# Retention block and expert layer on one core: group norm and residual of the last two items on another engine, one item stored in two parts, filler products and a new order at the end

## The chip, the core and the metric

The kernel runs on one NeuronCore of a Trainium2 chip. Five engines work side by side and meet only at semaphores: TensorE (PE) multiplies, VectorE (DVE) and ScalarE (ACT) do elementwise work and may read PSUM, GpSimd (POOL) does elementwise work in SBUF and issues the adding DMAs, SyncE (SP) issues the plain DMAs. The metric is the time of one launch in microseconds, the median of several runs.

## What is computed

The reference, cut to what matters. An item is one of the 8 batch entries of 512 tokens with 128 features. Four layers of the block run over 8 items, so the kernel counts 32 items, n = 0 to 31, with n = 8·layer + batch entry. The last three are 29, 30 and 31.

```python
xn = layernorm(x)                                   # (8, 512, 128)
def block(h, p):                                    # 4 layers
    r = retention(h, wk)                            # scores, row norm, times v
    a, gate = split(r @ w1 + b1)
    m = (a * silu(gate)) @ w2 + b2
    m = (m - mean(m over the item)) / sqrt(var + eps) * gg + gb    # group norm
    y = m + h                                       # residual
    f = gelu(y @ wf1 + bf1) @ wf2 + bf2
    return layernorm(f + y) * lg + lb
s = block x 4 (xn)
g = silu(moe(xn))                                   # 8 experts, one chosen per token
out = x + s * g
```

## The kernel before

The program is a software pipeline of steps. Step s handles the retention of item s, the gated product and group norm of item s-1, and the GELU product of item s-2; the layer norm of item s-3 follows. Tiles of the expert layer are woven between. Steps 0 to 29 are regular. After them each engine runs a hand-written list, its function `ending`, and since every engine runs its list strictly in that order, the lists fix which wait stands in front of which work. All that the change touches lies in these five lists and in the functions they call, from about 441 us of the profiled span on.

For an item n of the ending the chain is this. TensorE: `query`, `states`, `scores`, `outputs` (retention), `u_by_feature` (transposes), `late_value` and `late_gate` (first weight), `second_weight` (into bank 6; for item 31 `last_second_weight` in two halves into `pair`). Then the statistics of the group norm: sums over the free axis (ACT `group_sums` for items 29 and 30, DVE `last_sum_stats` and `last_group_sums` for 31), the sum over partitions by a product with a constant matrix (`late_means`), mean and variance on DVE (`late_gn_moments`), the power -1/2 on POOL (`gn_pow`), scale and shift per feature on DVE (`gn_shift`, three instructions of one column: gn_sc, gn_d, gn_bi). ACT's `residual` or `last_residual` writes scale·m + shift into y_sb, DVE's `y_residual` or `last_y` adds the input h (hT). TensorE's `gelu_first` reads y_sb, ACT's `gelu` reads its result, TensorE's `gelu_second` adds y and the second product (the tiles bank <- ident,y_sb and bank <- all_f,G_sb), and DVE takes the layer norm's statistics (`z_stats`, `z_moments`). POOL's `ln_pow` makes the factor.

For batch entries 0 to 4 the layer norm's result goes through `z_hat` (DVE, half of the rows), `layernorm` (ACT, the other half), POOL's `rows_scale` and `rows_shift` (times lg, plus lb), POOL's `scale` (times the SiLU of the expert layer, which lies in y_tok) and POOL's `store`, a DMA that adds to `out`, which was filled with x beforehand. For 5, 6 and 7, DVE prepares with `weigh("scale"|"bias"|"x", b)` the tensors g·lg, g·lb and x + g·lb, and after the statistics finishes with `centre` and `finish`, four passes of 128 columns each. Entry 5 is stored by an adding DMA of POOL, 6 and 7 by plain DMAs of SP, the last of which starts after `finish(31, 4, (2, 3))`.

The means of an item over all of its elements come, for the last items, as three columns from four products (mean, mean of squares, eps, minus the mean), so that DVE needs two instructions to the variance:

```python
mm(means_bank(n)[:, 0:1], mean[:, :], gs[:, 0:1], start=True, stop=True)        # L1619
mm(means_bank(n)[:, 1:2], mean[:, :], gs[:, 1:2], start=True, stop=False)       # L1620
mm(means_bank(n)[:, 1:2], mean_of[:, :], eps_sb[:, :], start=False, stop=True)  # L1621
mm(means_bank(n)[:, 2:3], less[:, :], gs[:, 0:1], start=True, stop=True)        # L1622
```

## Time and profile before

| | |
|---|---|
| median of 3 runs | 499.3 us (499.13 to 499.41) |
| the profiled execution | 499.69 us, of which the profile's span is 497.9 us |
| PE busy | 471.7 us (95%) |
| DVE busy | 369.5 us (74%) |
| ACT busy | 262.9 us (53%) |
| POOL busy | 258.5 us (52%) |

The profile gives for every instruction its start and duration, for idle time what ended it, and for any stretch the busy time of each engine with the clock that was granted to TensorE (PEclk; 1.00 is 2.4 GHz, 0.50 is 1.2 GHz). Times in the rows count from the span's start. A matmul of float32 stands as two instructions, so x4 are two products. A product's listed duration includes the time that it needs to drain; the distance of two starts is what it costs TensorE.

### The profile page before, as it was taken

Reading aid. Unit: us, or ns where it says so; the run is one execution under the profiler, and the core shown is the slowest. Engines: PE = TensorE matmul, PEld = TensorE weight load, DVE = VectorE, ACT = ScalarE, POOL = GpSimd, SP = SyncE. Lnnn points to the kernel's source line nnn. Section 1 sums busy time; section 2 is a strip of 40 time slices with the busy share of each in tenths; the row PEclk is TensorE's granted clock in tenths of the full one; section 3 lists DMA queues with packets and bytes.
Section 4 is the critical chain, followed back from the end, with each engine's and each line's share of the span. In section 5 each row is a group of like instructions: output and inputs, shape, how many; then the busy total and the mean of one; then the engine's idle time right before and its main releaser. Section 6 shows DMA issues by size and latency. Waiting matters only on the chain.

```text
span 497.9 us, 9900 instructions
## 1 busy us (share of the span) xinstructions
PE 471.7 (95%) x3167; PEld 395.3 (79%) x3167; DVE 369.5 (74%) x1326; ACT 262.9 (53%) x551; POOL 258.5 (52%) x289
## 2 busy tenths in 40 slices
PE   7999889998999999999999999999999999999964
PEld 5787566676898898898889889888988988876643
DVE  4758878887777676777767777867777786776866
ACT  3823344444564546665454666454466654488623
POOL 4520188888544555444455554454555455664551
PEclk9999999999999999999999999999999999999967
DMA  9999911111611111111111111110111100066034
GB/s 265 234 136 114 397 33 39 38 40 36 129 65 59 38 65 60 60 44 36 55 40 65 60 60 44 60 38 32 66 60 59 40 11 12 13 169 65 0 28 79
DMA packets 47393, 36.62 MB, mean 74 GB/s; under 512 B 13336, under 2 KB 38752, under 8 KB 47312
## 3 DMA queue, kind: packets, MB, share of 16 engines
q1 hardware_dynamic: 41376, 28.93, 22.9%
q0 software_dynamic: 5440, 6.28, 5.7%
q10 hardware_dynamic: 528, 0.79, 0.5%
q8 instruction: 27, 0.44, 0.4%
q14 instruction: 22, 0.18, 0.1%
HBM read 16.27 MB, written 10.99 MB: 55 GB/s over the span
## 4 chain that ended last, share of the span: by engine, by line
PE 71%; POOL 11%; DVE 8%; issue 6%; DMA 2%; ACT 1%; SPq 0%; DVEq 0%; POOLq 0%
PE bank L1595 9%; PE bank L1494 7%; PE bank L1478 7%; POOL x_slots L512 6%; PE pair L1687 4%; PE pair L1678 4%; PE pair L1644 4%; PE bank L1698 4%; PE bank L1505 4%; PE bank L1506 4%; PE bank L1507 4%; PE pair L1689 3%; PE pair L1639 3%; PE bank L1593 2%; PE bank L1533 2%
## 5 line engine op out<-in xcount | busy, mean ns | idle before, releaser
L546 POOL TENSOR_TENSOR zhat<-zhat,all_lg 128x512 f32<-128x512 f32 x29 | 38.6, 1332 | 80.3 <-PE bank L1551 73.9
L1595 PE MATMUL bank<-all_f,G_sb 128*128 128x128 f32 x512 | 74.5, 279 | 0.0
L1595 PEld LDWEIGHTS bank<-all_f,G_sb 128*128 128x128 f32 x512 | 68.9, 196 | 1.8 <-issue 1.7
L772 ACT ACTIVATE y_sb<-bank,gn_bi,gn_sc 128x512 f32<-128x512 f32 x31 | 24.1, 779 | 87.0 <-DVE gn_bi L1344 87.0
L745 ACT ACTIVATE uT_h<-bank 128x512 fp32r<-128x512 f32 x30 | 17.9, 598 | 92.8 <-PE bank L1561 92.8
L467 POOL TENSOR_TENSOR ln_rs<-ln_ve,half_neg 128x4 f32<-128x4 f32 x31 | 32.7, 1055 | 35.3 <-DVE ln_ve L871 35.1
L1478 PEld LDWEIGHTS bank<-moe_w,h_T 128*128 128x128 f32 x312 | 39.5, 191 | 14.0 <-issue 14.0
L659 ACT ACTIVATE h_T<-bank,w_t 128x128 f32<-128x128 f32 x156 | 44.6, 373 | 4.9 <-PE bank L1494 4.9
L593 POOL DMA_INDIRECT y_rows<-yt,slot_info x39 | 40.9, 1050 | 11.1 <-POOL yt L590 11.1
L716 ACT ACTIVATE G_sb<-bank,all_par 128x512 f32<-128x512 f32 x62 | 41.7, 694 | 9.3 <-PE bank L1533 7.0
L537 POOL TENSOR_TENSOR gn_rs<-gn_ve,half_neg 128x1 f32<-128x1 f32 x32 | 19.4, 607 | 49.5 <-DVE gn_ve L1210 40.3
L1494 PE MATMUL bank<-xtT,w_t 128*128 128x128 f32 x312 | 43.2, 281 | 0.0
L1478 PE MATMUL bank<-moe_w,h_T 128*128 x312 | 42.0, 278 | 0.0
L1133 DVE TENSOR_TENSOR rs<-pair,floor_sb 128x4 f32<-128x4 f32 x32 | 5.2, 162 | 47.3 <-PE pair L1689 46.3
L590 POOL TENSOR_SCALAR yt<-yt,slot_info 128x128 f32<-128x128 f32 x39 | 23.7, 608 | 30.3 <-DVE yt L1375 30.3
L554 POOL TENSOR_TENSOR htok<-zhat,all_lb 128x512 f32<-128x512 f32 x29 | 37.9, 1309 | 2.3
L1494 PEld LDWEIGHTS bank<-xtT,w_t 128*128 128x128 f32 x312 | 37.9, 192 | 0.0
L1689 PE MATMUL pair<-S_sb,q_sb 128*128 128x129 f32 x192 | 37.1, 275 | 0.0
L512 POOL DMA_INDIRECT x_slots<-xn,pos x32 | 32.6, 1019 | 8.1 <-issue 8.1
L1593 PE MATMUL bank<-ident,y_sb 128*128 128x128 f32 x128 | 35.6, 278 | 0.9 <-ACT G_sb L716 0.9
L1505 PE MATMUL bank<-uT_h,all_w 128*128 128x512 f32 x60 | 33.4, 557 | 1.7 <-DVE uT_l L1198 1.1
L1678 PE MATMUL pair<-q_sb,hT 128*128 128x128 f32 x256 | 34.0, 276 | 0.2 <-ACT q_sb L756 0.2
(227 smaller groups left out, 1249.2 us busy)
## 6 DMA issues: line engine op xcount, KB each, us to landing
w_t<-moe_w SPq DMA_DIRECT2D x39, 258.0 KB
x_slots<-moe_w SPq DMA_DIRECT2D x1, 2515.5 KB, 22.9
xt<-x_slots SPq DMA_DIRECT2D x39, 64.0 KB, 1.8
x_sb<-in_L_attn_x SPq DMA_DIRECT2D x8, 256.0 KB, 5.7
moe_w<-in_L_ffn_w SPq DMA_DIRECT2D x1, 2048.0 KB, 21.1
moe_w<-y_rows SPq DMA_DIRECT2D x8, 256.0 KB, 4.7
out<-in_L_attn_x SPq DMA_DIRECT2D x1, 1536.0 KB, 15.9
out<-moe_w POOLq DMA_DIRECT2D x6, 256.0 KB, 5.0
```

The costliest lines, as they stand in the source:

```text
L512: pool.indirect_dma_start(x_slots[:, :], bass.IndirectOffsetOnAxis(ap=pos[:, k:k + 1], axis=0), xn[:, k, :], None).then_inc(scattered, 16)
L546: pool.tensor_tensor(zhat[:, b % 2, :, :], zhat[:, b % 2, :, :], all_lg[:, li, :].unsqueeze(1).broadcast_to([P, C, D]), ALU.mult)\
L593: pool.indirect_dma_start(y_rows[:, :], bass.IndirectOffsetOnAxis(ap=slot_info[:, i, 0:1].bitcast(i32), axis=0), yt[ring(i)][:, :], None). ...
L659: last = act.activation(h_T[:, k * P:(k + 1) * P], bank[5][:, k * P:(k + 1) * P], ACT.Gelu, bias=w1_t[ring(i)][:, FF + k:FF + k + 1])
L716: act.activation(G_sb[:, k, :], f1_bank(n, k)[:, :], ACT.Gelu, bias=all_par[:, li, F_B + k:F_B + k + 1]).then_inc(G_done, 1)
L1478: last = mm(bank[5][:, 0:D], h_T[:, k * P:(k + 1) * P], moe_w2[:, bass.ds(e, 1), k, :].rearrange("p a d -> p (a d)"), start=k == 0, stop=k ...
L1494: last = mm(bank[5][:, k * P:(k + 1) * P], w1_t[ring(i)][:, k * P:(k + 1) * P], xtT[:, :], start=True, stop=True)
L1505: mm(dst[:, :], weights[:, 0, cols], high[:, :], start=True, stop=False)
L1593: mm(dst, y_sb[:, n % 2, at_c], ident[:, :], start=True, stop=False, is_transpose=True)
L1595: last = mm(dst, G_sb[:, k, at_c], all_f2[:, n // B, k, :], start=False, stop=k == 1)
L1678: last = mm(pair[:, 0, at_c], hT[:, n % B, at_c], q_sb[:, at_c], start=True, stop=True)
L1689: last = mm(dst, q_sb[:, c * P:(c + 1) * P], S_sb[:, c - 1, :], start=False, stop=True)
```

## The change

1. Group norm of items 30 and 31. DVE's `gn_shift` falls away for both. ACT makes gn_d (`centre_shift`), then gn_sc and gn_bi (`affine`), then writes h + shift into y_sb from SBUF (`shifted`); DVE's `late_y` and `last_y` read the product in PSUM, multiply it by gn_sc and add y_sb. Before, ACT read PSUM and DVE added two tensors in SBUF.
2. `late_means` is one product of two columns in place of four of one; DVE uses the three-instruction `gn_moments` for all items. Two constant matrices and their memsets at the start go.
3. Item 28 (batch entry 4): POOL makes g·lg and g·lb early (`weigh_scale`, `weigh_bias`) and adds g·lb to `out` by a DMA (`store_bias`); when the layer norm's result is there, one multiplication (`scale_rows`) and a second adding DMA (`store_rows`, which waits for the first to have landed) replace `rows_scale`, `rows_shift`, `scale(4)` and `store(4)`.
4. `keep_warm(1, bank[2])` after `last_second_weight` and `keep_warm(2, bank[2])` before `gelu_second(30)`: products of constants, 256 columns each, that nobody reads.
5. A new order of all lists. Of note: TensorE's `gelu_first(28)` goes ahead of `outputs(30)`, `late_means(31)` behind `gelu_first(30)`; DVE's `gn_shift(28)` and `y_residual(28)` ahead of `state_sums(30)`, `finish(29, 1)` from behind `z_stats(30)` to the front of `last_y(0)`; POOL's `gn_pow(28)` ahead of `store(0)`.

```diff
@@ constants @@
-        SILU = (0, 1, 2, 5, 4, 6, 3, 7)
-        SCALED = (0, 1, 2, 4, 3)
+        SILU = (0, 1, 2, 4, 5, 7, 6, 3)
+        SCALED = (0, 1, 2, 3)
@@ POOL @@
+            def weigh_scale(b):
+                pool.tensor_tensor(g_twice, y_twice, all_lg[:, L - 1, :]..., ALU.mult).then_inc(p_gl, 1)
+            def weigh_bias(b):
+                pool.tensor_tensor(y_twice, y_twice, all_lb[:, L - 1, :]..., ALU.mult).then_inc(p_gl, 1)
+            def store_bias(b):
+                pool.wait_ge(out_seeded, 16)
+                pool.dma_start(out[b]..., y_twice, accum_op=ALU.add).then_inc(bias_added, 16)
+            def scale_rows(n):
+                pool.wait_ge(z_done, n + 1)
+                pool.tensor_tensor(zhat[:, b % 2, :, :], zhat[:, b % 2, :, :], g_twice, ALU.mult).then_inc(p_gl, 1)
+            def store_rows(n):
+                pool.wait_ge(bias_added, 16)
+                pool.dma_start(out[b]..., zhat[:, b % 2, :, :], accum_op=ALU.add).then_inc(out_done, 16)
             def ending():
                 scale(0)
+                gn_pow(28)
+                store(0)
+                ln_pow(27, 3)
                 scale(1)
                 scale(2)
-                store(0)
-                gn_pow(28)
+                weigh_scale(4)
+                weigh_bias(4)
+                store_bias(4)
+                gn_pow(29)
                 store(1)
-                store(2)
-                ln_pow(27, 3)
-                gn_pow(29)
-                ln_pow(28, 4)
                 rows_scale(27)
                 rows_shift(27)
+                ln_pow(28, 4)
+                store(2)
+                scale(3)
                 gn_pow(30)
-                rows_scale(28)
-                rows_shift(28)
-                scale(4)
+                store(3)
+                scale_rows(28)
+                ln_pow(29, 5)
                 gn_pow(31)
-                scale(3)
-                store(4)
-                ln_pow(29, 5)
-                store(3)
+                store_rows(28)
+                store(5)
                 ln_pow(30, 6)
-                store(5)
@@ ACT @@
+            def centre_shift(n):
+                act.activation(gn_d[:, :], gn_m[:, 0:1], ACT.Identity, bias=all_par[..., W2_B], scale=-1.0)
+            def affine(n):
+                act.wait_ge(gn_rstd, n + 1)
+                if n == LAST:
+                    act.wait_ge(y_done, LAST)
+                act.activation(gn_sc[:, :], gn_rs[:, :], ACT.Copy, scale=all_par[..., GN_G])
+                act.activation(gn_bi[:, :], gn_d[:, :], ACT.Identity, bias=all_par[..., GN_B], scale=gn_sc[:, :])
+            def shifted(n, part):
+                act.activation(y_sb[:, n % 2, part], hT[:, n % B, part], ACT.Identity, bias=gn_bi[:, :])
...
                 table(ACT.Gelu, 2)
+                layernorm(*late(28, 3))
                 gelu(*late(29, 2))
-                layernorm(*late(28, 3))
-                residual(*late(30, 1))
+                centre_shift(30)
+                affine(30)
+                shifted(30, slice(0, S))
                 gelu(*late(30, 2))
-                last_residual(0)
-                last_residual(1)
+                centre_shift(31)
+                affine(31)
+                shifted(31, slice(0, HALF))
+                shifted(31, slice(HALF, S))
                 last_gelu(0)
@@ DVE @@
+                dve.scalar_tensor_tensor(y_sb[:, LAST % 2, part], pair[:, half, 0:HALF], gn_sc[:, :],
+                                         y_sb[:, LAST % 2, part], ALU.mult, ALU.add).then_inc(y_done, 1)
+            def late_y(n):
+                dve.wait_ge(gn_done, n + 1)
+                dve.scalar_tensor_tensor(y_sb[:, n % 2, :], bank[6][:, :], gn_sc[:, :], y_sb[:, n % 2, :], ...)
...
                 gated(31)
-                late_gn_moments(30)
-                weigh("x", 7)
-                gn_shift(*late(30, 1))
+                gn_moments(*late(30, 1))
                 last_sum_stats(0)
                 last_sum_stats(1)
-                y_residual(*late(30, 1))
+                weigh("bias", 6)
                 last_group_sums()
+                weigh("x", 6)
+                late_y(30)
+                weigh("x", 7)
                 z_stats(*late(29, 2))
-                late_gn_moments(31)
                 z_moments(*late(29, 2))
-                weigh("bias", 6)
+                gn_moments(*late(31, 1))
                 centre(29)
-                gn_shift(*late(31, 1))
-                weigh("bias", 5)
+                finish(29, 1)
                 last_y(0)
-                weigh("x", 6)
                 last_y(1)
                 z_stats(*late(30, 2))
                 z_moments(*late(30, 2))
-                finish(29, 1)
                 centre(30)
+                finish(30, 2)
@@ TensorE @@
-                mm(means_bank(n)[:, 0:1], mean[:, :], gs[:, 0:1], start=True, stop=True)
-                mm(means_bank(n)[:, 1:2], mean[:, :], gs[:, 1:2], start=True, stop=False)
-                mm(means_bank(n)[:, 1:2], mean_of[:, :], eps_sb[:, :], start=False, stop=True)
-                mm(means_bank(n)[:, 2:3], less[:, :], gs[:, 0:1], start=True, stop=True).then_inc(pe_gn, 1)
+                mm(means_bank(n)[:, 0:2], mean[:, :], gs[:, :], start=True, stop=True).then_inc(pe_gn, 1)
...
                 scores(30)
+                gelu_first(*late(28, 2), 0)
+                gelu_first(*late(28, 2), 1)
+                outputs(30)
                 parts_value(29)
-                outputs(30)
-                second_weight(29)
...
                 last_second_weight(1)
+                keep_warm(1, bank[2])
                 gelu_second(*late(29, 2))
-                late_means(31)
                 gelu_first(*late(30, 2), 0)
                 gelu_first(*late(30, 2), 1)
+                late_means(31)
+                keep_warm(2, bank[2])
                 gelu_second(*late(30, 2))
```

## Rows read from the trace of the kernel before

**Rows 1.** Stretches of the ending: busy us (instructions) by engine, granted clock, DMA
```profile
472.93:475.92 2.99, 0.01 (x1) 0.00 (x0) 2.75 (x8) 0.78 (x1) 1.68 (x2) 0.97 0.01 3
475.92:482.28 6.36, 5.49 (x12) 2.91 (x13) 4.18 (x20) 1.52 (x3) 3.96 (x5) 0.50 0.01 0
482.28:486.49 4.21, 4.21 (x21) 4.21 (x22) 1.36 (x3) 0.77 (x2) 1.71 (x2) 0.56 1.21 122
486.49:491.00 4.51, 4.16 (x28) 3.42 (x27) 4.38 (x23) 3.25 (x7) 2.25 (x2) 1.00 0.04 5
```

**Rows 2.** TensorE in order of time: start, us, line, tiles, idle before
```profile
444.49 0.28 PE L1607 MATMUL bank<-gs,mean_all 128*128 128x2 f32 x2
...
457.59 0.28 PE L1619 MATMUL bank<-gs,mean_all 128*128 128x1 f32 x2
...
458.40 1.10 PE L1666 MATMUL bank<-uT_sb,last_w 128*128 128x512 f32 x2
...
466.24 1.88 PE L1533 MATMUL bank<-y_sb,all_f 128*128 128x512 f32 x4
...
469.58 1.13 PE L1704 MATMUL pair<-gg_sb,all_w 128*128 128x256 f32 x4 [0.68 <-DVE gg_sb L1122]
...
475.92 0.59 PE L1619 MATMUL bank<-gs,mean_of 128*128 128x1 f32 x2 [2.99 <-DVE gs L1161]
...
477.65 3.76 PE L1533 MATMUL bank<-y_sb,all_f 128*128 128x512 f32 x4
...
486.31 1.89 PE L1540 MATMUL bank<-y_sb,all_f 128*128 128x256 f32 x8
```

**Rows 3.** DVE in order of time around group norm 30
```profile
468.79 0.74 DVE L1122 SCALAR_TENSOR_TENSOR gg_sb<-bank,all_par,th_sb 128x512 f32<-128x512 f32 x1
...
469.76 0.68 DVE L1061 TENSOR_TENSOR moe_w<-moe_w,x_sb 128x512 f32<-128x512 f32 x1
470.89 1.22 DVE L1339 TENSOR_TENSOR gn_sc<-gn_rs,all_par 128x1 f32<-128x1 f32 x1 [0.44 <-POOL gn_rs L537]
...
472.21 1.24 DVE L1344 SCALAR_TENSOR_TENSOR gn_bi<-gn_d,gn_sc,all_par 128x1 f32<-128x1 f32 x1
...
475.23 0.20 DVE L1175 BATCH_NORM_AGGREGATE gs_mv<-gs_st 128x2 f32<-128x12 f32 x1
```

**Rows 4.** POOL in order of time
```profile
448.47 3.19 POOL L530 DMA_DIRECT2D out<-moe_w  x2
...
469.93 0.93 POOL L537 TENSOR_TENSOR gn_rs<-gn_ve,half_neg 128x1 f32<-128x1 f32 x1 [0.57 <-DVE gn_ve L1191]
470.82 1.27 POOL L546 TENSOR_TENSOR zhat<-zhat,all_lg 128x512 f32<-128x512 f32 x1
...
478.32 0.55 POOL L537 TENSOR_TENSOR gn_rs<-gn_ve,half_neg 128x1 f32<-128x1 f32 x1 [3.57 <-DVE gn_ve L1191]
```

**Rows 5.** ACT in order of time
```profile
449.72 0.20 ACT L699 ACTIVATE table_of<-ones 128x1 f32<-128x1 f32 x1
...
466.68 1.28 ACT L699 ACT_TABLE_LOAD   x1
...
468.08 1.25 ACT L716 ACTIVATE G_sb<-bank,all_par 128x512 f32<-128x512 f32 x2
469.22 0.81 ACT L682 ACTIVATE zhat<-bank,ln_nb,ln_rs 128x128 f32<-128x128 f32 x2
473.49 0.78 ACT L772 ACTIVATE y_sb<-bank,gn_bi,gn_sc 128x512 f32<-128x512 f32 x1 [3.46 <-DVE gn_bi L1344]
```

**Rows 6.** DVE's last stretch, in order of time
```profile
486.51 0.89 DVE L861 BATCH_NORM_STATS2 ln_st<-bank 128x6 f32<-128x128 f32 x4 [2.52 <-PE bank L1595]
...
487.96 1.14 DVE L1087 SCALAR_TENSOR_TENSOR moe_w<-xn,ln_rs,moe_w 128x128 f32<-128x128 f32 x4
...
494.36 0.61 DVE L1087 SCALAR_TENSOR_TENSOR moe_w<-xn,ln_rs,moe_w 128x128 f32<-128x128 f32 x2
```

**Rows 7.** The adding stores of POOL (line 530): us from issue to landing
```profile
DMA to landing us min/median/max: 4.6/5.0/6.1
```

More of the change, by code:

```diff
@@ L818, in ending @@
                 queries(*late(30, 0))
+                residual(*late(28, 1))
                 gate(*late(29, 1))
                 table(ACT.Gelu, 0)
-                residual(*late(28, 1))
-                group_sums(29, L - 1)
+                gelu(*late(28, 2))
+                table(ACT.Silu, 1)
+                silu(4)
+                silu(5)
                 queries(*late(31, 0))
                 u_whole(30)
-                gelu(*late(28, 2))
-                table(ACT.Silu, 1)
-                silu(5)
+                silu(7)
+                silu(6)
+                group_sums(29, L - 1)
                 layernorm(*late(27, 3))
                 gate_silu(30)
-                silu(4)
-                silu(6)
                 residual(*late(29, 1))
                 silu(3)
-                silu(7)
                 u_whole(31)
@@ L1309, in ending @@
                 z_moments(*late(30, 2))
-                finish(29, 1)
                 centre(30)
+                finish(30, 2)
                 last_stats(0)
                 last_moments(0)
-                finish(30, 2)
                 last_stats(1)
@@ L1778, in ending @@
                 u_by_feature(*late(30, 0))
-                gelu_first(*late(28, 2), 0)
-                gelu_first(*late(28, 2), 1)
+                states(31)
+                second_weight(29)
                 scores(31)
-                states(31)
                 late_value(30)
+                late_gate(30)
                 late_means(29)
-                late_gate(30)
                 outputs(31)
```

95 lines of the change are left out of this document (54 added, 41 removed).

## Prediction

> **What bounds the kernel now.** I read the stretches of the ending by engine first, then TensorE's instructions in order of time, then DVE, POOL and ACT around the one long gap. Up to 472.9 us TensorE is nearly always busy and bounds the kernel; the change leaves that part's products alone except for the order. Then TensorE stands still for 2.99 us until DVE has the sums of item 31 [rows 2], and when it starts again its clock is granted at half, 0.50, where it had been full: the stretch 475.92 to 482.28 runs at 0.50 and the next, to 486.49, at 0.56; only after 486.49 is it 1.00 again [rows 1]. Four products that last 1.88 us at full clock (466.24) last 3.76 us (477.65) [rows 2]. Behind them DVE is the last engine: from 486.51 to 494.97 it hardly stops [rows 6]. So the ending has three parts: TensorE to the start of `last_second_weight` at 469.58 [rows 2]; a serial chain of group norm, with the slow clock at its end, to the end of `gelu_second(30)`; and DVE's tail.
>
> Why is the gap so long? gn_sc is one column, which should be about nothing, and yet lasts 1.22 us, and gn_bi 1.24 us; POOL's multiplication of 512 columns begins at 470.82, lasts 1.27 us, and its next one follows [rows 3, 4]. Both DVE instructions end when a POOL instruction ends. They have two inputs in SBUF. An instruction of DVE with one input in PSUM (468.79, 0.74 us) ran at the usual length beside POOL's work of that time [rows 3]. So DVE's small instructions are held by POOL's large ones, which costs the chain (1.22 - 0.15) + (1.24 - 0.22), about 2.1 us. The reverse holds too: POOL's power of one column lasts 0.55 us at 478.32, when DVE left it alone, and 0.93 at 469.93, beside the DVE instruction of 469.76 [rows 3, 4].
>
> **The change, part by part.**
>
> *Products for the means.* Four products cost TensorE 458.40 - 457.59 = 0.81 us; the one product of two columns stands in the rows of item 28 with 0.28 us of length and 0.14 us to the next start [rows 2]. For items 29 and 30 this lies on TensorE's bound part: 2 x 0.67 = 1.3 us gained. For item 31 the four fell in the half clock (475.92 to 477.65, 1.73 us [rows 2]); that goes with the chain below. DVE's third instruction (0.15 us) is the price, once on the chain.
>
> *New order up to 468 us.* `gelu_first(28)` before `outputs(30)` delays the retention of item 30, since TensorE now waits for y of item 28, but the same work has been done by the time `scores(31)` ends. `y_residual(28)` and `gn_shift(28)` stand before `state_sums(30)` on DVE; queued behind them are the mask and the sums, for which TensorE waits only after the 1.7 us of `gelu_first(28)`, which covers them; without this cover it would be some 1.5 us. The earlier `gn_pow(28)` avoids a wait there. I take 0, with -0.4 to +0.6 as bounds. So `last_second_weight` starts at about 469.6 - 1.3 = 468.3.
>
> *Group norm of item 30.* ACT has to get through `gate_silu(31)` and the table load (1.28), layer norm 28 (0.8) and the two GELU passes of item 29 (1.25), as before [rows 5]; all this sat before 470.0 in the old trace and does so again, about 469.9. The power comes behind `scale(3)` on POOL and ends at about 469.6, at 0.55 in place of 0.93. A one-column ACT instruction lasts 0.20 us [rows 5]; two chained ones cost about 0.45, against 0.15 + 0.22 on DVE unheld, and over 2.4 as they were. `shifted(30)` costs as much as the residual did, about 0.78 less 0.1 of overlap [rows 5], so h + shift is there at 471.1. `late_y(30)` has its larger input in PSUM and costs the 0.74 of the PSUM form [rows 3]. But before it DVE has the statistics of item 31, `weigh("bias", 6)` and `weigh("x", 6)` (0.68 us long [rows 3], some 0.60 from start to start): 468.3 + 1.1 for the product, + 0.7 + 0.6 + 0.6 + 0.6, about 472.0. `weigh("x", 6)` has two inputs in SBUF and meets POOL's `scale_rows(28)`, which follows the power and a store and lasts 1.27: held to its end, up to 1 us more. I take this, since the hold is what the rows show at every such meeting: late_y(30) ends at 473.6 (bounds 472.6 and 474.2).
>
> *TensorE after that.* `gelu_first(30)` at full clock: 1.72 + 0.15, to 475.4; ACT's second pass ends 0.8 to 0.9 later, and `gelu_second(30)` starts at 476.4, where it was 482.3: 5.9 us earlier. `keep_warm(1)` and `(2)` cost 0.45 and 0.90 us of TensorE from the 128x256 products (1.89 us for eight instructions, four products [rows 2]). Both lie in waits: the first for ACT's GELU of item 29 (at 469.8), the second for that of item 30, which ends 0.8 us after the products. If the covers were gone they would cost 1.35; I take 0.1. TensorE's longest wait is then some 1.5 us (before `gelu_first(30)`) where it was 2.99. Waits of 0.68 us and the like left the clock full [rows 1, 2]; none of about 1.5 us is shown. I take the clock as full. `gelu_second(30)` then lasts 2.2 us and not 4.2 [rows 1]: it ends at 478.8.
>
> By the Trainium skill (TensorE: Matmul & The Clock Gate, Part 1) the chip grants the clock by how busy TensorE has been, half being the default. This trace agrees with its fall after the 2.99 us gap. By that rule the filler products are of use only so far as they raise the busy share, and they don't touch the 1.5 us wait, which lies before `gelu_first(30)`; if that wait were enough the clock would fall all the same, the second case below.
>
> *Item 31.* `late_means(31)` stands behind `gelu_first(30)`, so its mean comes at about 475.7, later than it could; then 0.6 on DVE, `ln_pow(29)` and `gn_pow(31)` on POOL (1.0 + 0.55), ACT's two small ones and two halves, and `last_y` ends its two halves at 479.2. That is 0.4 us behind `gelu_second(30)`, and this is what is late next.
>
> *The tail.* Before, 494.97 - 486.51 = 8.46 us on DVE from the first statistics [rows 6]. `finish(29, 1)`, 1.14 us long and 1.06 from start to start [rows 6], moves ahead into a wait. `finish(30)` may then wait 0.1 us for the last power, and the last statistics 0.3 us for TensorE. 479.2 - 478.8 + 8.46 - 1.06 + 0.4 = 8.2 after the end of `gelu_second(30)`, hence an end at 487.0 if all goes against it and 486.5 with the small gaps between instructions that overlap; I take 486.7. What follows (last transfer, end of the program) stays: 497.9 - 494.97 = 2.9 us.
>
> *Item 28 in two stores.* POOL does three passes of 512 columns as before, but two of them early, and one store more. Each store holds POOL about 1.6 us (two in 3.19 [rows 4]). The early one stands before `gn_pow(29)`, which has over 1 us of slack. The late one stands behind `gn_pow(31)`, lands within 6.1 us of its issue [rows 7], at about 483.5, and nobody waits for it; its wait for the first store, landed since 463, costs nothing. The two memsets at the start are 0.2 us on an engine that waits for DVE there.
>
> **Sum.** 494.97 - 486.7 = 8.3 us: means 1.3; hold of DVE and slow clock between 470 and 482, together 4.6 (5.9 less those 1.3); `gelu_second(30)` at full clock 2.0; tail 0.4 (1.06 less new waits and `last_y`). The profiled execution took 499.69 and would take 491.4; the median is 0.4 below it, so 499.3 - 8.3 = **491.0 us**.
>
> **The rivals.**
> 1. *As forecast*, chance 0.62: 491.0, own range 489.6 to 492.6 (bounds of late_y, order and POOL's stores).
> 2. *The clock falls all the same* after the waits around `late_y(30)`, chance 0.18. For: the small waits lie close together, and no row shows a wait of 1.5 us with the clock full after it. Against: TensorE is busy over 80% from 466 to 479. Price: of 4 us of products up to the end of `gelu_second(30)` nearly 3 us go twice as long, some covered: +3.0, 494.0 (493 to 495).
> 3. *No hold, and less waiting*: `scale_rows(28)` comes before or after the weighing, late_y is 1 us earlier, chance 0.13: 489.9, down to 489.2.
> 4. *The change doesn't do what it says*: the filler products are irrelevant because the shorter gap by itself keeps the clock. That gives the same 491.0; it is inside case 1 and only an experiment can tell it.
> 5. *Slower*: POOL becomes the bound by its stores, chance 0.04. In the new list `store(1)` and `store(2)` stand before `gn_pow(30)`, and `store_rows(28)` and `store(5)` before the last `ln_pow(30)`. At 1.6 us each they fit. Should each hold POOL for 4 us, most of the way to its landing (4.6 at least [rows 7]), two of them delay gn_pow(30) by 4.8 less 0.9 of slack, and the others delay `gn_pow(31)` and `ln_pow(30)` by another 5.4 in all: +9.3, 500.3. From 3.9 us a store on, the kernel is slower. Against: the stores in the rows take 1.6 us, with DVE busy beside them. The Trainium skill (SBUF — State Buffer, section on the bandwidth-pool intuition) gives 3.1 us for such a DMA beside a DVE copy, for 0.62 alone; by that the sum would be some 495.5. The trace has 1.6.
>
> What is left, 0.03, is a smaller gain for no reason seen here, 495 to 499.
>
> **Range and chances.** A measurement of this kernel can tell some 0.2% (1 us) from no change. The range takes case 1 with its bounds, case 3 and most of case 2: 489.2 to 494.4. Faster 0.94, within 0.2% 0.02, slower 0.04.
>
> **What would show it.** Right: gn_sc and gn_bi on ACT for items 30 and 31 at 0.2 us each; the clock 1.00 in every stretch to the last product; `gelu_first(30)` 1.9 us long and starting at 473 to 474.5; `last_second_weight` at 468 to 468.7; DVE's last instruction at about 487. Wrong: a granted clock of 0.50 anywhere before 482; a POOL store over 2.5 us before a power; TensorE waiting over 2 us before `gelu_first(30)`; `last_second_weight` not earlier than before, which would say that the order costs what the means gain.

## The result, and the profile of the changed kernel

The changed kernel takes 495.39 us (median of 7 runs, 494.12 to 496.74); the kernel before took 497.72 us beside it (median of 7, 496.62 to 499.41). The ratio is 0.9942, with a 95% interval of 0.992 to 0.9964. It is faster, but by 2.3 us where 8.3 were forecast, and 495.39 lies above the range, which ended at 494.4. The profiled execution of the changed kernel took 494.12 us (span 492.4, clock 0.999), the fastest of its 7 and the only one with a mean clock above 0.994; that of the kernel before took 499.69.

First the same view as [rows 1], stretches of the ending: busy us (instructions) by engine in the order PE, PEld, DVE, ACT, POOL, then the granted clock and DMA.

```profile
444.00:462.80 18.80, 17.82 (x110) 13.45 (x107) 16.34 (x44) 13.65 (x25) 13.00 (x11) 1.00 0.33 33
462.80:465.35 2.55, 0.01 (x1) 0.01 (x1) 2.41 (x7) 1.23 (x2) 1.26 (x1) 1.00 0.61 72
465.35:474.86 9.51, 8.97 (x42) 5.74 (x42) 8.29 (x22) 7.53 (x17) 6.94 (x6) 1.00 0.42 42
474.86:476.71 1.85, 0.00 (x1) 0.00 (x1) 1.78 (x6) 0.00 (x0) 0.00 (x0) 1.00 0.59 73
476.71:483.70 6.99, 6.84 (x37) 5.33 (x38) 6.61 (x31) 3.54 (x9) 4.17 (x4) 1.00 0.24 22
```

In this execution the half clock of [rows 1] is gone: 1.00 in every stretch. But TensorE now stands still twice, for 2.55 and for 1.85 us, and DVE is busy in both. TensorE in order of time (as [rows 2]; in brackets the idle time before and who ended it):

```profile
465.35 0.66 PE L1614 MATMUL bank<-ident,u_sb 128*128 128x128 f32 x4 [2.59 <-DVE u_sb L1197]
...
470.37 1.11 PE L1753 MATMUL pair<-gg_sb,all_w 128*128 128x256 f32 x4
...
472.45 0.30 PE L1646 MATMUL bank<-ident,y_sb 128*128 128x128 f32 x1 [0.54 <-ACT G_sb L753]
...
476.71 1.99 PE L1586 MATMUL bank<-y_sb,all_f 128*128 128x512 f32 x4 [1.85 <-DVE y_sb L1245]
...
482.15 1.99 PE L1593 MATMUL bank<-y_sb,all_f 128*128 128x256 f32 x8
```

The 2.59 us wait before `u_by_feature(31)` has no counterpart in the kernel before. It puts `last_second_weight` at 470.37, later than the 469.58 of [rows 2]. What DVE did meanwhile (as [rows 3]):

```profile
460.21 2.54 DVE L1392 TENSOR_TENSOR gn_sc<-gn_rs,all_par 128x1 f32<-128x1 f32 x1
...
462.86 1.22 DVE L1397 SCALAR_TENSOR_TENSOR gn_bi<-gn_d,gn_sc,all_par 128x1 f32<-128x1 f32 x1
...
471.86 2.96 DVE L1114 TENSOR_TENSOR moe_w<-moe_w,all_lb 128x512 f32<-128x512 f32 x1
...
475.91 0.75 DVE L1245 SCALAR_TENSOR_TENSOR y_sb<-bank,gn_sc,y_sb 128x512 f32<-128x512 f32 x1
...
489.49 0.61 DVE L1144 SCALAR_TENSOR_TENSOR moe_w<-xn,ln_rs,moe_w 128x128 f32<-128x128 f32 x2
```

and POOL beside it (as [rows 4]):

```profile
460.14 1.28 POOL L528 DMA_DIRECT2D out<-moe_w  x1
460.95 1.78 POOL L581 TENSOR_TENSOR zhat<-zhat,all_lg 128x512 f32<-128x512 f32 x1
462.81 1.26 POOL L589 TENSOR_TENSOR htok<-zhat,all_lb 128x512 f32<-128x512 f32 x1
...
471.75 1.30 POOL L528 DMA_DIRECT2D out<-moe_w  x1
472.57 1.70 POOL L559 TENSOR_TENSOR zhat<-zhat,xn 128x512 f32<-128x512 f32 x1
```

This is group norm of item **29**, not 30. Its gn_sc, one column, ends at 462.75, when `rows_scale(27)` ends (462.73); its gn_bi ends at 464.08, when `rows_shift(27)` ends (464.07). `weigh("bias", 6)` ends at 474.82, some 0.55 us after `scale_rows(28)` (474.27), which is about what the work itself takes from start to start. In the trace of the kernel before the same gn_sc of item 29 met no POOL instruction:

```profile
460.04 0.16 DVE L1339 TENSOR_TENSOR gn_sc<-gn_rs,all_par 128x1 f32<-128x1 f32 x1 [0.44 <-POOL gn_rs L537]
```

The chain of work that ended last (start, us, what) runs through all three held instructions. The piece called issue is the third: the weighing is not waiting for anything that the profile shows.

```profile
460.26 2.50 DVE gn_sc L1392
462.86 1.22 DVE gn_bi L1397
...
472.01 2.73 issue
```

ACT's small instructions (as [rows 5]) are there, but longer than the 0.20 us that the forecast gave each:

```profile
472.18 0.30 ACT L768 ACTIVATE gn_d<-gn_m,all_par 128x1 f32<-128x1 f32 x1
472.37 0.30 ACT L776 ACTIVATE gn_sc<-gn_rs,all_par 128x1 f32<-128x1 f32 x1
472.71 0.39 ACT L778 ACTIVATE gn_bi<-gn_d,all_par,gn_sc 128x1 f32<-128x1 f32 x1
```

`shifted(30)` was ready at 473.85, two us before `late_y(30)` got to run (475.91), so this cost nothing. DVE ends at 490.10, where 486.7 was forecast and 494.97 was before [rows 6].

### The profile page after: what moved, and what is told of

The parts are those of the page before. It is cut to its first block, busy times and chain, and to the rows that moved or that the text cites. A ratio compares the mean times of both kernels' runs of the same rounds, so it can differ in the third digit from the quotient of the medians.

```text
span 492.4 us, 9882 instructions
## 1 busy us (share of the span) xinstructions
PE 465.9 (95%) x3155; PEld 390.9 (79%) x3155; DVE 371.7 (75%) x1323; ACT 264.5 (54%) x557; POOL 258.6 (53%) x288
## 4 chain that ended last, share of the span: by engine, by line
PE 69%; POOL 10%; DVE 9%; issue 7%; DMA 2%; ACT 2%; SPq 0%; POOLq 0%; DVEq 0%
PE bank L1648 8%; PE bank L1547 7%; PE bank L1531 7%; POOL x_slots L510 5%; PE pair L1727 4%; PE pair L1736 4%; PE bank L1747 4%; PE pair L1693 4%; PE bank L1558 4%; PE bank L1559 4%; PE bank L1560 4%; PE pair L1738 3%; PE pair L1688 3%; PE bank L1614 2%; PE bank L1586 2%
## 5 line engine op out<-in xcount | busy, mean ns | idle before, releaser
L1648 PE MATMUL bank<-all_f,G_sb 128*128 128x128 f32 x512 | 72.9, 275 | 0.0
L1648 PEld LDWEIGHTS bank<-all_f,G_sb 128*128 128x128 f32 x512 | 67.3, 192 | 1.7 <-issue 1.7
L572 POOL TENSOR_TENSOR gn_rs<-gn_ve,half_neg 128x1 f32<-128x1 f32 x32 | 18.1, 566 | 44.9 <-DVE gn_ve L1264 44.7
L589 POOL TENSOR_TENSOR htok<-zhat,all_lb 128x512 f32<-128x512 f32 x28 | 36.5, 1304 | 2.2
```

Source lines behind the costliest of these rows:

```text
L589: pool.tensor_tensor(htok[:, b * C:(b + 1) * C, 0:D], zhat[:, b % 2, :, :], all_lb[:, li, :].unsqueeze(1).broadcast_to([P, C, D]), ALU.add)\
L1648: last = mm(dst, G_sb[:, k, at_c], all_f2[:, n // B, k, :], start=False, stop=k == 1)
```

## Experiments

My theory from the two traces: the loss is DVE held by POOL, at group norm 29 and again at `weigh("bias", 6)`, and the store that stands directly ahead of POOL's multiplication makes each hold longer. The rivals: the order as such is too slow, whoever stands where; POOL's work is too much; the idle products or the one-product means gave nothing; the clock is what decides. Fourteen kernels bear on them. Each is timed beside the kernel before on the same chip, and ratios are to that. All compute the full reference. Where the quoted texts say A and B, these are the theory and the rival of that run.

### How much of it is the clock, and how much one execution tells

Three kernels: the one before, unchanged; the one after, unchanged; and the one before with six idle products in TensorE's long wait.

```
 gelu_second(*late(29, 2))
+keep_warm(6, bank[2])
 late_means(31)
```

> The kernel before, unchanged, for the clock and the spread of its own executions beside the others of this call. Theory A (half clock after the long wait of TensorE in every execution): ratio 1.00, mean granted clock about 0.985 in each execution, spread of the times caused by how long the half clock lasts. Rival B (the clock is the same in all, the spread has another source): times differ at equal clock.

> The changed kernel, unchanged, on the same chip as the other three. Theory A: its executions fall into groups by granted clock, near 0.999 with a span about 492.4 us, near 0.994 with about 1 us more, and lower with more; ratio to before 0.992 to 0.996. Rival B: times do not follow the clock. A trace with a clock under 0.999 should show where the half clock lies: in products (costs time) or behind the last product (costs nothing).

> Before plus six idle products of 256 columns in TensorE's wait for the means of item 31, nothing else changed. If the half clock costs what the rows of before say (gelu_first(30) 1.9 us, gelu_second(30) 2.0 us, four mean products 0.8 us): the span is 4 to 4.7 us shorter, about 493.5, with the clock 1.00 until the last product. If the chain on DVE and ACT hides it, less than 1 us.

Measured: before unchanged 498.2 us (496.53 to 499.9, 12 runs), ratio 1.0007 [0.9986, 1.0028]. After unchanged 496.39 (495.45 to 497.32, 12 runs), 0.9958 [0.9941, 0.9975]. Before with idle products 495.2 (495.06 to 495.55, 6 runs), 0.9931 [0.9911, 0.9951].

The kernel before is not one time but several: its executions lie near 496.5 us at a mean clock of 0.992 or 0.993, near 498 at 0.985 to 0.991, and near 499.8 at 0.981 to 0.985. The profile on which I had made the sum (499.69) is of the last kind. In the profile of the new execution the clock stayed at half for a shorter time (stretches of two us, columns as in the first view):

```profile
476.00:478.00 2.00, 2.00 (x10) 1.44 (x11) 1.59 (x12) 0.00 (x0) 0.51 (x1) 0.80 0.04 8
478.00:480.00 2.00, 2.00 (x3) 0.34 (x1) 1.96 (x9) 0.69 (x1) 2.00 (x3) 0.50 0.00 0
480.00:482.00 2.00, 1.13 (x9) 0.93 (x9) 1.08 (x3) 1.60 (x3) 2.00 (x3) 0.85 0.36 26
```

`gelu_second(30)` starts there at 481.10, where it was 482.28. With idle products TensorE's wait before the means of item 31 shrinks from 3.00 to 0.41 us and `gelu_first(30)` runs at full clock:

```profile
472.73 2.76 PE L1429 MATMUL bank<-ones,ident 128*128 128x256 f32 x12
475.90 0.38 PE L1619 MATMUL bank<-gs,mean_of 128*128 128x1 f32 x2 [0.41 <-DVE gs L1161]
...
476.81 1.96 PE L1533 MATMUL bank<-y_sb,all_f 128*128 128x512 f32 x4
```

So one added line is worth 2.9 us in the median (498.13 to 495.2), more than the whole change gives (2.3 us in the result, 1.7 here), and the runs then lie within 0.5 us. What the clock costs the median execution is 2.9 us; the profiled one lost more.

The changed kernel isn't free of the clock either. Of its 12 executions six lie near 495.6 us (mean clock 0.994) and six near 497.2 (0.987 to 0.991), none near the 494.12 of the first profile. In its second profile, of an execution of 495.73 us, the waits are the same (2.59, 0.53, 1.85 us), and yet the clock falls after the last of them:

```profile
478.00:480.00 2.00, 2.00 (x6) 0.98 (x5) 0.93 (x8) 0.92 (x2) 0.94 (x1) 0.53 0.00 0
480.00:482.00 2.00, 2.00 (x8) 1.58 (x9) 1.90 (x9) 1.33 (x5) 1.05 (x3) 0.61 0.03 8
```

### Are the idle products of use in the changed kernel?

```
 last_second_weight(1)
-keep_warm(1, bank[2])
 gelu_second(*late(29, 2))
...
 late_means(31)
-keep_warm(2, bank[2])
```

> After without its three idle products. If they are what keeps the clock at full (theory A): the granted clock falls to 0.50 behind the 1.85 us wait before gelu_first(30) in many executions and the time is 2 to 4 us over after. If the shorter wait by itself keeps the clock (my case 4): the same time as after within 0.5 us.

Measured: 496.28 us (494.23 to 498.19, 12 runs), 0.9953 [0.9934, 0.9972]. Beside the 496.39 of the changed kernel this is no difference. In the one profile of it the clock fell after the wait before `u_by_feature(31)`, here 2.60 us, which comes before any idle product (466 to 468 us at 0.66, the next two us at 0.50); a fall at that place they can't prevent. It stayed at 1.00 behind the longer wait of 2.85 us before `gelu_first(30)`. Without them the spread is wider, 4 us where it was 1.9.

### The stores ahead of POOL's multiplications

Two ways to take the pair of store and multiplication apart. In the first `store(2)` follows `store(1)`, so that gn_shift(29) should meet two stores:

```
 gn_pow(29)
 store(1)
+store(2)
 rows_scale(27)
 rows_shift(27)
 ln_pow(28, 4)
-store(2)
```

> After with POOL's store(2) moved up behind store(1), so that two stores and not one stand between gn_pow(29) and rows_scale(27). In the trace of after gn_sc of item 29 starts at 460.21, 0.07 us after store(1), lasts 2.54 us and ends with rows_scale(27), though that is listed as starting only at 460.95. Theory A (a store directly ahead of a POOL multiplication stretches the hold to the whole pair): gn_sc lasts about 3.4 to 3.9 us, TensorE's wait before u_by_feature(31) grows from 2.6 to about 3.6 us, the kernel is about 1 us slower. Rival B (only the multiplication holds, from its listed start on): gn_sc runs at 0.15 us beside the stores, gn_bi and all three are done before the multiplication starts; the wait shrinks to under 0.5 us and the kernel is about 2 us faster.

In the second both stores go behind the multiplications:

```
 gn_pow(29)
-store(1)
 rows_scale(27)
 rows_shift(27)
+store(1)
 ln_pow(28, 4)
...
-store(3)
 scale_rows(28)
+store(3)
```

> After with store(1) moved behind rows_shift(27) and store(3) behind scale_rows(28). Theory A: gn_sc of item 29 is held by rows_scale(27) alone, 1.2 us in place of 2.54, gn_bi 1.2 us as before; weigh(bias, 6) 1.7 us in place of 2.96. TensorE's wait before u_by_feature(31) 1.3 us in place of 2.6, the wait before gelu_first(30) about 0.6 us in place of 1.85: time 2 to 2.6 us under after. Rival B (the store holds DVE wherever it stands): the hold sits elsewhere and the time stays within 0.7 us of after.

The second gives 491.39 us (491.26 to 491.52, 4 runs), 0.9867 [0.9833, 0.9901]: 4 to 5 us less than the changed kernel, from moving two lines. Expected were 2 to 2.6. Profile against profile it is 2.9 (494.12 to 491.26). The rest goes with the clock: most executions of the changed kernel take 1 to 3 us more than its profiled one, at a lower mean clock, and these four lie within 0.3 us of each other. DVE, POOL and TensorE of it:

```profile
460.00 1.22 DVE L1392 TENSOR_TENSOR gn_sc<-gn_rs,all_par 128x1 f32<-128x1 f32 x1
...
470.35 1.61 DVE L1114 TENSOR_TENSOR moe_w<-moe_w,all_lb 128x512 f32<-128x512 f32 x1
```

```profile
459.94 1.26 POOL L581 TENSOR_TENSOR zhat<-zhat,all_lg 128x512 f32<-128x512 f32 x1
```

```profile
473.84 1.98 PE L1586 MATMUL bank<-y_sb,all_f 128*128 128x512 f32 x4 [0.51 <-DVE y_sb L1245]
```

gn_sc is held for 1.22 us instead of 2.54, the weighing for 1.61 instead of 2.96. TensorE's wait before `u_by_feature(31)` goes from 2.59 to 1.28, that before `gelu_first(30)` from 1.85 to 0.51. `last_second_weight` starts at 468.85, `gelu_first(30)` at 473.84 (forecast 473.6), and DVE's last instruction ends at 487.22 (forecast 486.7). This is nearly the kernel that I had forecast (491.0). That the time agrees to 0.4 us is in part luck: DVE ends 0.5 us late, and what follows it takes 2.3 us and not 2.9.

The first gives 493.16 us (493.01 to 494.89, 6 runs), 0.9907 [0.988, 0.9934], also faster than the changed kernel, where theory A had it 1 us slower with a hold of over 3.4 us, and by about what rival B had. But it has a row that I can't explain. DVE, then POOL:

```profile
460.21 0.16 DVE L1392 TENSOR_TENSOR gn_sc<-gn_rs,all_par 128x1 f32<-128x1 f32 x1
...
460.48 1.17 DVE L1397 SCALAR_TENSOR_TENSOR gn_bi<-gn_d,gn_sc,all_par 128x1 f32<-128x1 f32 x1
```

```profile
460.14 2.60 POOL L528 DMA_DIRECT2D out<-moe_w  x2
461.71 2.32 POOL L581 TENSOR_TENSOR zhat<-zhat,all_lg 128x512 f32<-128x512 f32 x1
```

gn_sc and gn_d run free beside the stores, but gn_bi is held until 461.65, before the multiplication is listed as started. Is it a store that holds, or the multiplication, earlier than it is listed? The wait before `u_by_feature(31)` is 0.17 us, but `last_second_weight` starts only at 469.60, after 1.45 us of waiting for `gated(31)`: the holds now fall on the statistics of item 28 (1.28 us at 464.12, 1.13 at 466.92). The weighing stays at 2.61 us, since `store(3)` stood where it was.

### A store alone

To tell that apart: `store(1)` stays directly behind `gn_pow(29)`, but the multiplication must wait until DVE is through with u of item 31. `store(3)` goes behind `scale_rows(28)`.

```
 gn_pow(29)
 store(1)
+pool.wait_ge(u_done, LB)
 rows_scale(27)
 rows_shift(27)
 ln_pow(28, 4)
...
-store(3)
 scale_rows(28)
+store(3)
```

> After with store(3) behind scale_rows(28), and with rows_scale(27) made to wait for normalise_u(31), so that the only POOL work beside DVE's gn_shift(29) is store(1) itself, with no multiplication in POOL's queue that may run. Theory A (the multiplication behind a store is what holds; the store alone holds nothing): gn_sc, gn_d and gn_bi of item 29 last 0.15, 0.15 and 0.22 us, TensorE's wait before u_by_feature(31) is under 0.3 us, the time is 1 us or more under the 491.4 us of the stores behind. Rival B (a store holds DVE's two-input instructions too, as gn_bi beside the two stores suggests, 1.17 us): one of the three lasts over 0.8 us beside store(1).

Measured: 490.57 us (490.44 to 491.18, 4 runs), 0.9852 [0.9828, 0.9875]. DVE, then POOL:

```profile
460.52 0.16 DVE L1393 TENSOR_TENSOR gn_sc<-gn_rs,all_par 128x1 f32<-128x1 f32 x1
460.60 0.15 DVE L1395 TENSOR_TENSOR gn_d<-all_par,gn_m 128x1 f32<-128x1 f32 x1
460.79 0.22 DVE L1398 SCALAR_TENSOR_TENSOR gn_bi<-gn_d,gn_sc,all_par 128x1 f32<-128x1 f32 x1
```

```profile
460.45 1.29 POOL L528 DMA_DIRECT2D out<-moe_w  x1
462.31 1.27 POOL L581 TENSOR_TENSOR zhat<-zhat,all_lg 128x512 f32<-128x512 f32 x1 [0.57 <-DVE u_sb L1198]
```

All three run at their own length beside the store: with no multiplication ready behind it, the store holds nothing. The hold of 2.54 us in the changed kernel needs the multiplication behind the store, and begins before that is listed as started (gn_sc at 460.21, `rows_scale(27)` at 460.95). TensorE's wait before `u_by_feature(31)` is gone, although `rows_scale(27)` starts 1.36 us later than in the changed kernel: POOL had the slack. That also answers, for this place, the rival by which POOL's work is too much.

### Moving the held instruction

The weighing that was held for 2.96 us goes behind `late_y(30)`:

```
-weigh("bias", 6)
 last_group_sums()
-weigh("x", 6)
 late_y(30)
+weigh("bias", 6)
+weigh("x", 6)
 weigh("x", 7)
```

> After with DVE's weigh(bias, 6) and weigh(x, 6) moved behind late_y(30), nothing else. If the 2.96 us of weigh(bias, 6), held by POOL's scale_rows(28), is what delays late_y(30) and with it gelu_first(30): late_y(30) starts at about 473.9 (when ACT's h + shift is there) and not 475.91, the wait before gelu_first(30) is 0 and not 1.85 us, and about 1.5 to 2 us are gained at gelu_second(30), less what the weighing costs behind it (up to 1.2 us before the statistics of item 31): 0.8 to 2 us under after. If the hold was not on the path: the same as after.

Measured: 494.74 us (493.98 to 495.53, 6 runs), 0.9935 [0.9908, 0.9963]; the changed kernel has 0.9942 and 0.9958, so a gain of 0.3 to 1.1 us by the ratios, where 0.8 to 2 was expected. The hold didn't go, it moved to the next instruction with two inputs in SBUF, one column in `last_group_sums()`:

```profile
472.42 2.06 DVE L1215 TENSOR_TENSOR gs<-gs_mv,all_par 128x1 f32<-128x1 f32 x1
```

`gelu_first(30)` starts at 475.46 in place of 476.71, but the weighing is now due later: a new wait of 1.47 us stands before `last_gelu_first(31)` (at 482.22, as late as in the changed kernel).

Then the same with group norm of item 29 on ACT as well (`centre_shift(29)`, `affine(29)`, `shifted(29)` for `residual(29)` on ACT; `late_y(29)` for `gn_shift(29)` and `y_residual(29)` on DVE).

> As the one before, and group norm 29 done as the change does 30 and 31 (ACT makes scale and shift, DVE's late_y reads PSUM), so that no one-column instruction of DVE with two SBUF inputs stands before normalise_u(31). If the holds at 460.21 (2.54 us) and 462.86 (1.22 us) cause the 2.6 us wait of TensorE before u_by_feature(31): that wait falls to under 0.4 us, last_second_weight starts at about 468 as I forecast (470.37 in after), and the kernel is 3.5 to 4.5 us under after, about 491. If something else sets it, less than 2 us.

Measured: 493.25 us (493.11 to 495.2, 5 runs), 0.9922 [0.9892, 0.9953], where 491 was expected. The wait before `u_by_feature(31)` is gone as expected. But `late_y(29)` stood behind the statistics of item 28 (it starts at 464.09), and TensorE now waits 1.91 us for it before `second_weight(30)`; the hold of 2.07 us at `last_group_sums()` and the 1.47 us at `last_gelu_first(31)` stay.

### Single parts

On the kernel before, with its six idle products, the one-product means alone (and DVE's `gn_moments` with them):

```
-mm(means_bank(n)[:, 0:1], mean[:, :], gs[:, 0:1], start=True, stop=True)
-mm(means_bank(n)[:, 1:2], mean[:, :], gs[:, 1:2], start=True, stop=False)
-mm(means_bank(n)[:, 1:2], mean_of[:, :], eps_sb[:, :], start=False, stop=True)
-mm(means_bank(n)[:, 2:3], less[:, :], gs[:, 0:1], start=True, stop=True)
+mm(means_bank(n)[:, 0:2], mean[:, :], gs[:, :], start=True, stop=True)
```

> Before with the six idle products, and the one-product means for items 29, 30 and 31 in place of four products, so that the granted clock does not blur it. My forecast priced the two means on TensorE's bound part at 1.3 us. If right: last_second_weight starts about 1.2 us earlier than with the idle products alone (469.54) and the time is 1.2 to 1.9 us under the 495.2 of that kernel. Rival (DVE, held by POOL before gated(31), sets the start of last_second_weight): under 0.5 us.

Measured: 494.21 us (494.1 to 494.38, 5 runs), 0.9915 [0.9888, 0.9942], so 1.0 us less than with four products. I had priced 1.3 us for items 29 and 30. In the trace only 0.55 of it reaches `last_second_weight` (469.54 to 468.99): TensorE's wait there for `gated(31)` grows from 0.68 to 1.35 us. The gain is swallowed by the next engine; the rest of the 1.0 comes from item 31.

On the fast order (both stores behind), group norm of items 30 and 31 back on DVE, as before:

> After with the stores behind the multiplications (491.4 us), and with group norm and residual of items 30 and 31 done as before (DVE scale and shift, ACT from PSUM, DVE adds in SBUF). Theory A (two-input instructions of DVE are held by POOL's multiplications): gn_sc of item 30 meets scale_rows(28) and is held about 1.2 us, late_y's place is reached 1 to 2 us later, the kernel takes 492.5 to 493.5. Rival B (the move to ACT is worth nothing, since ACT's small instructions cost 0.3 to 0.4 us each where DVE's cost 0.15 to 0.22): 491 to 491.6.

Measured: 493.25 us (493.05 to 493.55, 4 runs), 0.9894 [0.9858, 0.9929], 1.9 us more than 491.39. gn_sc of item 30 is held again (1.08 us at 471.07), and TensorE waits 0.84 us before `gelu_first(30)` and 1.17 before `last_gelu_first(31)`. So ACT's group norm is worth 1.9 us, once the stores are out of the way.

On the fast order without the three idle products (the edit as above):

> After with the stores behind the multiplications and without the three idle products. TensorE's waits are then 1.3, about 1.0 and 0.5 us in place of 2.6, 0.55 and 1.85. If short waits keep the clock by themselves: full clock in every execution, 491.4 us as with the products. If the idle products are needed: executions with a clock under 0.995 and 1 to 3 us more.

Measured: 491.67 us (491.49 to 492.11, 4 runs), 0.9861 [0.9826, 0.9896]; 0.3 us more than with them. The single waits are at most 1.3 us there; the four executions lie within 0.6 us at mean clocks of 0.995 to 0.998, and in the profile the clock falls only behind the last product. The idle products of this change are worth nothing to 0.3 us.

Item 28 as before, in the changed kernel (three passes after the layer norm and one store):

```
-weigh_scale(4)
-weigh_bias(4)
-store_bias(4)
...
 store(3)
-scale_rows(28)
+rows_scale(28)
+rows_shift(28)
+scale(4)
 ln_pow(29, 5)
 gn_pow(31)
-store_rows(28)
+store(4)
```

> After with item 28 as before: rows_scale(28), rows_shift(28), scale(4) and one store in place of the two early weighings, scale_rows(28) and two stores. The forecast priced this part at nothing. If it is off the path: 495.4 to 496.4 us as after. If the POOL passes matter through their holds: weigh(bias, 6) still meets store(3) and rows_scale(28) (2.96 us), then two more passes of 1.27 us each stand in POOL's queue, weigh(x, 6) is held by the next, gelu_first(30) starts 1 us later, and the early weighings of item 5 and 7 on DVE are no longer slowed; 0.5 to 2 us slower than after.

Measured: 498.88 us (498.37 to 500.09, 10 runs), 1.0016 [1.0002, 1.0031]: without this part the change would be no gain at all. It is worth 2.5 to 3.5 us. DVE and TensorE:

```profile
473.63 3.05 DVE L1113 TENSOR_TENSOR moe_w<-moe_w,all_lb 128x512 f32<-128x512 f32 x1
...
476.83 0.98 DVE L1214 TENSOR_TENSOR gs<-gs_mv,all_par 128x1 f32<-128x1 f32 x1
...
477.98 1.68 DVE L1117 TENSOR_TENSOR moe_w<-moe_w,x_sb 128x512 f32<-128x512 f32 x1
```

```profile
480.38 3.47 PE L1585 MATMUL bank<-y_sb,all_f 128*128 128x512 f32 x4 [4.46 <-DVE y_sb L1244]
```

With three POOL multiplications in a row, three DVE instructions are held one after the other (0.6 us of work in the first, 0.16 in the second, 0.6 in the third), all of them ahead of `late_y(30)`. TensorE waits 4.46 us and its clock falls to 0.50 behind that. In this profile it had already been at 0.59 and 0.56 from 466 to 470 us, so part of the 2.5 to 3.5 us can be the clock; how much was not measured.

The same run shows where a hold begins that covers a store. Group norm of item 29, DVE, then POOL:

```profile
460.34 0.15 DVE L1391 TENSOR_TENSOR gn_sc<-gn_rs,all_par 128x1 f32<-128x1 f32 x1
460.41 2.51 DVE L1393 TENSOR_TENSOR gn_d<-all_par,gn_m 128x1 f32<-128x1 f32 x1
```

```profile
460.24 1.34 POOL L528 DMA_DIRECT2D out<-moe_w  x1
461.09 1.80 POOL L581 TENSOR_TENSOR zhat<-zhat,all_lg 128x512 f32<-128x512 f32 x1
```

gn_sc is through at 460.49, gn_d is not and stays until the multiplication ends (462.89). So the hold begins some 0.25 us behind the start of the store and over 0.5 us ahead of the listed start of the multiplication. In the changed kernel, ln_nb of item 28 (two SBUF inputs, four columns) stands beside `store(2)` with `scale(3)` directly behind it, and is through 0.23 us after the store's start (468.22, 0.16 us): not held. The limit isn't known to better than a few hundredths of a us, since gn_sc of the changed kernel, due to be through 0.23 us behind its store as well (460.37), was held.

### The best version

Both stores behind, group norm 29 on ACT too, and `late_y(29)` directly behind `normalise_u(31)`, the place that the miss of the run above pointed to:

```
 gated(30)
-gn_shift(*late(29, 1))
 normalise_u(31)
+late_y(29)
 z_stats(*late(28, 2))
 z_moments(*late(28, 2))
-y_residual(*late(29, 1))
```

> A version meant to beat both: after, with the stores behind the multiplications and group norm 29 on ACT too, late_y(29) right behind normalise_u(31). No one-column instruction of DVE with two SBUF inputs is left before normalise_u(31), so TensorE's 1.3 us wait before u_by_feature(31) should fall under 0.4 us, and last_second_weight start at 467.5 to 468. If the rest follows: 490.0 to 490.8 us. If ACT's or DVE's order behind it takes the gain: 491 to 491.6.

Measured: 490.09 us (490.02 to 490.12, 4 runs), 0.9831 [0.9796, 0.9866], faster than both kernels; 1.3 us less than with the stores behind alone. No wait before `u_by_feature(31)`, and `gelu_first(30)` waits 0.35 us. DVE ends at 486.00. Whether the other way to spare item 29 (the multiplication that waits, 490.57) adds to this was not tried.

## Why the prediction was wrong

**The mechanism was right; where it would strike was read for one place only.** The prediction names DVE held by POOL as the cause of the long gap, and plans for up to 1 us at `weigh("x", 6)`. Three of its terms failed: the order, taken as 0; the hold ahead of `late_y(30)`, taken too small; and the clock, taken as full. The first and largest is "New order up to 468 us", costed at 0 with bounds of -0.4 to +0.6. It asks what is queued behind each moved DVE step, and never lays POOL's new list beside DVE's new list. The diff puts `store(1)`, `rows_scale(27)` and `rows_shift(27)` directly behind `gn_pow(29)`, and the instructions that `gn_pow(29)` releases are just gn_shift(29). By the rule of the prediction itself that is a hold of some 2 us (1.22 - 0.15 + 1.24 - 0.22) [rows 3]; it was 3.4. TensorE waits 2.59 us and `last_second_weight` starts at 470.37, not 468.3: 2.1 us of the error.

**The size of the second hold.** From `last_second_weight` to the end of `late_y(30)` the forecast had 5.3 us, with 1 us of hold; it took 6.3 (470.37 to 476.66), since `weigh("bias", 6)` was held from the moment that `store(3)` had started: 2.96 us in place of 0.6, with the small statistics and `weigh("x", 6)` then unheld. 1.0 us of error, a term of the sum mis-sized. What shows it: with the store behind, the same instruction takes 1.61 us, and then the forecast start of `gelu_first(30)` comes true within 0.3 us. Together 2.1 + 1.0, and 0.3 from there to the end of DVE, are the 3.4 us by which DVE ended late (490.10, not 486.7). What follows DVE took 2.3 us, 0.6 less than the 2.9 before, and so the profiled execution was 494.12 and not 491.4.

**The scale.** The sum was made on one execution, taken to be 0.4 us above the median. It was of the slowest kind, and so were the three runs behind the 499.3; the four beside the changed kernel took 496.62 to 497.72. Over all 7 the median is 497.72, 2.0 below the profiled 499.69. The profiled execution of the changed kernel is the fastest of its 7, 1.3 below the median. So 5.6 us between the two profiles are 2.3 between the medians. This, 3.3 us, is the larger part of the 6.0 us by which the gain was missed; the steps inside the profiled execution are the other 2.7. The gain at TensorE's clock was the price in that execution, 4.4 us (DVE's end at 494.97, and at 490.55 with six idle products). In the median the same edit gives 2.9, and part of it isn't kept, since the clock still falls in executions of the changed kernel.

**Means.** 1.3 us forecast for items 29 and 30. Alone, 0.55 us of it reached `last_second_weight`, the rest became a longer wait for `gated(31)`; with item 31 it was 1.0. Over-priced by not asking what is late next, which for the other steps was asked. (What the prediction calls four products of 1.88 us are four listed instructions, two products; its sum used the length and not the count.)

**Order, without the hold.** Take the hold away (the multiplication that waits), and there is no wait before `u_by_feature(31)` and `last_second_weight` starts at 468.17, where 468.3 was forecast: with the means, "0" was right for the rest of the order.

**Item 28 in two stores** was costed at nothing. It is worth 2.5 to 3.5 us: without it three holds in place of one stand ahead of `late_y(30)`. The forecast had the effect inside its sum (one hold of 1 us ahead of `late_y(30)`), under the name of group norm 30; what ACT gives to that by itself, measured with the stores behind, is 1.9 us. POOL's stores themselves lasted 1.3 us each, under the 1.6 that were taken, and no power waited for one: the mechanism of the slower rival did not occur. The stores did harm all the same, by what they do to the hold of DVE, which no rival had. (That rival's 495.5 for stores of 3.1 us does not fit its own 500.3 for stores of 4: 0.9 us less for each of four stores gives 496.7. Nothing hung on it.)

**ACT.** Forecast 0.20 us for each one-column instruction; 0.30 with one operand of one column per partition, 0.39 with two. The row of 0.20 was of an instruction without such an operand. The Trainium skill (ScalarE: Activation LUTs, What ACT_TABLE_LOAD costs) adds about 0.09 us for each; this trace agrees, 0.20, 0.30 and 0.39. It cost nothing here, since DVE was late.

**The clock.** "TensorE waits over 2 us before `gelu_first(30)`" did not come (1.85), and in the recorded profile the clock was 1.00 throughout. But "I take the clock as full" failed for the median. In the second profile the clock was at 0.53 and 0.61 between 478 and 482 us, a sign that the prediction names as wrong, and DVE ended at 491.72 and not 490.10. Six of the 7 executions, and all 12 of the later ones, have a mean clock of 0.994 or less and are 1 to 3 us slower than the profiled 494.12, which by itself lies inside the range. So it is the clock that carries the median out of it, and the rival by which it falls all the same (chance 0.18, 493 to 495) comes nearest to what was measured. The place of the fall was seen in one of these executions only. The rival by which the idle products are irrelevant was right as to them: nothing in the changed kernel, 0.3 us with the stores behind.

**What the forecast got right**, once the two holds are taken down: `last_second_weight` 468.85 (forecast 468 to 468.7, so 0.15 late, with a hold of 2.1 us still at group norm 29), `gelu_first(30)` 473.84 (473 to 474.5), end of DVE 487.22 (about 487), median 491.39 (491.0).

**Open**: what held gn_bi for 1.17 us with two stores ahead of the multiplication. A hold that begins over 0.5 us before the multiplication is listed explains the 2.54 us, but not this one, which ends before the listed start. Two stores in a row don't hold by themselves either: in the kernel before, gn_sc, gn_d and gn_bi of item 28 lasted 0.15, 0.15 and 0.22 us from 449.23 on, beside two stores (448.47, 3.19 us). And why the same waits leave the clock at 1.00 in one execution of the same kernel and at 0.53 in the next.

## What to carry to other kernels

When an order is rewritten, lay the new lists of the two engines that can hold each other side by side, over the whole stretch and not only at the old gap, and look above all at what the releasing instruction is followed by on its own queue. A hold that is moved or shortened is not gone until no instruction of the sensitive kind stands beside it. Price a clock or any other state of the chip from many executions, with the cheapest edit that removes it alone, before a large change is credited with it.

## What the runs showed of the hardware

- A POOL multiplication of 512 columns holds a DVE instruction with two SBUF inputs until its own end, even one of a single column: that took 1.08 to 1.24 us where it takes 0.15 to 0.22 alone. I had taken this from the old trace. The Trainium skill (SBUF — State Buffer, Who interferes with whom) states it as an exclusive lock on ports that the two engines share; the traces agree.
- With a store directly ahead of the multiplication the hold covers most of the store too: 2.54 and 2.96 us for instructions of 0.16 and 0.68 us. What is through within some 0.25 us of the store's start can escape it (0.15 and 0.16 us). With the multiplication kept waiting, the store holds nothing (0.16, 0.15, 0.22 us beside a store of 1.29). None of this stood in the prediction.
- In the run with two stores DVE's `ln_ve` of four columns, one SBUF input, took 1.28 us at 464.12 instead of 0.17, until the end of `rows_shift(27)` (464.11 for 1.26). So the kind that can be held is wider than two SBUF inputs.
- One kernel has several times by how long its clock stays at half: 495.5 to 500.1 us in 29 executions of the one before. Six idle products made that 495.06 to 495.55.
